# A recurrent time-mixing stage: another order on VectorE, three operations on GpSimd, and the last batch's end inside the stage behind it

## The chip, the core and the metric

The kernel runs on one core of a Trainium2 chip. A core has TensorE (PE in the profile, with PEld for its weight loads), VectorE (DVE), ScalarE (ACT), GpSimd (POOL) and a queue for transfers (SP), each with its own instruction stream; they meet only at semaphores. The metric is the device time of one launch in microseconds; the numbers below are medians of runs on the chip, and one execution was profiled.

## The reference

Two layers are computed for x of shape (4, 512, 128), which is 4 batches of 512 tokens with 128 channels:

```python
x = x + time_mix(layernorm(x))                 # RWKV-v4 recurrence, then W_out
x = x + transformer(layernorm(x))              # 6 layers: windowed attention and gated MLP
# time mixing: r, v, k = layernorm(x) @ W_rvk.T ; per channel, over the tokens t:
p = max(pp, u + k_t);   e1, e2 = exp(pp - p), exp(u + k_t - p)
y_t = (e1 * aa + e2 * v_t) / (e1 * bb + e2)
p2 = max(pp + w, k_t);  aa, bb, pp = exp(pp+w-p2)*aa + exp(k_t-p2)*v_t, ..., p2
out = (sigmoid(r) * y) @ W_out.T
```

The transformer part projects q, k and v for 16 heads, normalises and rotates q and k, attends in windows of 32 tokens, and runs a gated MLP; this is done 6 times.

## The kernel before

The program has two blocks of code, one behind the other, and every engine goes from the first to the second only when all engines have ended the first. The order of the instructions on each engine is written out by hand.

**The first block is time mixing.** It works on whole batches, with the 128 channels on the partitions and the 512 tokens along the free axis, so that one operation covers 128x512 elements in float32. For batch b VectorE normalises the rows (statistics, layer_norm), PE turns and projects them (turn_x, project), and ScalarE copies the results out (take_x, take_k, take_vr). Then VectorE runs three scans along the tokens, which are the recurrence: pp (scan_maximum, which also makes the exponents xd and yd), and bb and aa (scan_state, which first multiplies e2 by v into e2v). ScalarE makes e1, e2, f1 and f2 of the exponents (exponentials). The quotient takes six products and sums on VectorE (weigh_output: f2v, f1b, f1a, den, num and den again, with sigmoid's denominator er) and divide (a reciprocal and a product, rwkv). PE multiplies by W_out (output), VectorE adds x (residual, x_res), and the second LayerNorm follows: centre on PE, squares and a copy on ScalarE (take_centred), the variances on PE, an initial guess on VectorE (seed), Newton's steps on GpSimd (newton, twelve small operations), the widening to 128 columns on PE (widen), and a product on VectorE (scale_state) that leaves x_state[:, b], the transformer's input.

The batches are pipelined: pass b of VectorE's loop holds scale_state of b-2, scan_state of b, scan_maximum of b+1, residual of b-1, weigh_output of b, seed of b-1 and divide of b. GpSimd meanwhile splits the transformer's weights into two parts (w_hi and w_lo, one TENSOR_SCALAR and one TENSOR_TENSOR for each of the six chunks), and multiplies the rotation tables. In the loop it waits for the semaphore den2_ready before each split; this is given by the last operation of weigh_output, ahead of the reciprocal:

```python
for b in range(BATCH):                       # GpSimd, L302
    pool.wait_ge(den2_ready, b + 1)
    weights.split(pool, 0, 2 + b)
    newton(b - 1)
```

Behind the loop stands the end of the last batch, 3: scale_state(2), residual(3), the root on VectorE itself, scale_state(3) (L447 to L453), with centre and widen on PE.

**The second block is the transformer.** It goes in steps of 128 tokens of one batch in one layer, 4 steps for a batch, 96 steps and 10 more to empty the pipeline. A step projects six chunks of 512 columns on PE (V0, Q0, Q1, K0, K1, V1, three matmuls each, L1248 to L1250). For each q or k chunk, VectorE multiplies the bank by two tables (rotate, L921 and L928), ScalarE squares it (L1107), VectorE sums the squares (L938), and then there is one root for the whole step (L957 to L965). GpSimd adds the two products (L808) and normalises (L816). Scores, softmax, weighting, output projection and the MLP of earlier steps lie between them. In the first two steps those are not there yet. Batch 3 is first read in step 10.

## Time and profile before

| what | us |
|---|---|
| median of 3 runs (1739.13 to 1754.56) | 1740.24 |
| the profiled execution | 1745.12 |
| its span | 1743.3 |
| last operation of time mixing on VectorE ends | 102.47 |
| first projection of the transformer starts | 107.84 |

The profiled execution is 4.88 us above the median, and 1.82 us of it lie outside its span. Over the whole span PE is busy 91%, VectorE 83%, ScalarE 64% and GpSimd 60%. These are shares over both blocks: the first 108 us have limits of their own, and of the whole page only rows of that stretch tell about them.

### The profile page before, as it was taken

What the parts mean: (1) busy time and instruction counts of PE and PEld (TensorE: products, weight loads), DVE (VectorE), ACT (ScalarE), POOL (GpSimd) and SP (SyncE); (2) the same over time, 40 slices, a digit from 0 to 9 for tenths busy, and PEclk for the clock granted to TensorE, in tenths of its full rate; (3) what the DMA queues carried; (4) which work ended last, traced back from release to release, by engine and by line L of the source; (5) the groups of instructions that cost most, each with busy time, mean ns of one, the idle gap of its engine ahead of it and who ended that gap; (6) DMA issues with size and microseconds to landing.
All of it is one profiled execution on the core that took longest, in us unless ns stands there. A gap on an engine that the chain in (4) does not pass through costs nothing.

```text
span 1743.3 us, 77091 instructions
## 1 busy us (share of the span) xinstructions
PE 1585.1 (91%) x32733; PEld 1276.4 (73%) x32733; DVE 1445.9 (83%) x3193; ACT 1116.5 (64%) x2014; POOL 1049.6 (60%) x1028
## 2 busy tenths in 40 slices
PE   5358999999999999999999999999999999999985
PEld 2137878778778777778777787778777887787863
DVE  8758989888889888888888889888888888888851
ACT  5226667667667666667666666667666766776752
POOL 2236766666766665667566567576577585675530
PEclk8569999999999999999999999999999999999996
DMA  2011111111111111110211111211111211011110
GB/s 85 31 32 51 37 49 37 57 42 48 32 49 37 58 43 38 40 49 28 67 30 51 41 37 40 61 36 51 38 39 40 59 39 48 24 47 52 32 38 13
DMA packets 41083, 75.05 MB, mean 43 GB/s; under 512 B 9472, under 2 KB 22568, under 8 KB 40744
## 3 DMA queue, kind: packets, MB, share of 16 engines
q1 hardware_dynamic: 40744, 70.12, 13.9%
q8 instruction: 263, 4.31, 1.0%
q14 instruction: 76, 0.62, 0.1%
HBM read 20.08 MB, written 2.10 MB: 13 GB/s over the span
## 4 chain that ended last, share of the span: by engine, by line
PE 74%; issue 9%; DVE 5%; ACT 4%; POOL 3%; ACTq 0%; DVEq 0%; POOLq 0%
PE bank L1258 8%; PE bank L1248 8%; PE bank L1362 8%; PE bank L1295 7%; PE wide L1333 7%; PE bank L1250 7%; PE bank L1249 7%; PE bank L1348 5%; PE bank L1417 4%; PE bank L1313 4%; PE bank L1405 2%; PE bank L1284 2%; PE bank L1407 2%; PE bank L1406 2%; POOL qk L808 1%
## 5 line engine op out<-in xcount | busy, mean ns | idle before, releaser
L816 POOL TENSOR_TENSOR qk<-qk,rnorm 128x512 f32<-128x512 f32 x384 | 401.9, 1047 | 351.9 <-DVE rnorm L965 351.9
L808 POOL TENSOR_TENSOR qk<-qk,qk_sin 128x512 f32<-128x512 f32 x384 | 492.5, 1283 | 166.7 <-DVE qk_sin L928 166.5
L1107 ACT ACTIVATE squares<-bank 128x512 f32<-128x512 f32 x384 | 229.4, 598 | 153.8 <-DVE qk_sin L928 153.7
L938 DVE TENSOR_REDUCE norm<-squares 128x8 f32<-128x512 f32 x384 | 258.3, 678 | 31.0 <-ACT squares L1107 28.9
L1248 PE MATMUL bank<-w_hi,xs_hi 128*128 128x512 f32 x576 | 262.5, 456 | 16.1 <-ACT squares L1107 7.2
L921 DVE TENSOR_TENSOR qk<-bank,tables 128x512 f32<-128x512 f32 x384 | 261.7, 682 | 7.9 <-PE bank L1250 7.1
L928 DVE TENSOR_TENSOR qk_sin<-bank,tables 128x512 f32<-128x512 f32 x384 | 261.1, 680 | 0.6 <-POOL qk L808 0.6
L1250 PE MATMUL bank<-w_hi,xs_lo 128*128 128x512 f32 x576 | 230.7, 401 | 0.0
L1249 PE MATMUL bank<-w_lo,xs_hi 128*128 128x512 f32 x576 | 228.9, 397 | 1.4 <-issue 1.4
L1258 PE MATMUL bank<-ident,qk 128*128 128x128 f32 x1536 | 226.5, 278 | 3.3 <-POOL qk L816 2.0
L1258 PEld LDWEIGHTS bank<-ident,qk 128*128 128x128 f32 x1536 | 181.1, 142 | 42.8 <-issue 3.3
L1362 PE MATMUL bank<-o_t,w_o_s 128*128 128x128 f32 x1536 | 192.4, 279 | 2.8 <-DVE probs L979 1.9
L1295 PE MATMUL bank<-k_t,q_t 64*32 64x64 f32 x12288 | 152.1, 224 | 42.9 <-issue 42.6
L971 DVE TENSOR_REDUCE row_max<-bank 128x8 f32<-128x512 f32 x192 | 123.7, 686 | 75.8 <-PE bank L1295 74.4
L1362 PEld LDWEIGHTS bank<-o_t,w_o_s 128*128 128x128 f32 x1536 | 181.0, 193 | 6.0 <-issue 4.8
L1295 PEld LDWEIGHTS bank<-k_t,q_t 64*32 64x32 f32 x12288 | 143.0, 105 | 55.3 <-issue 50.5
L1333 PEld LDWEIGHTS wide<-v,p_t 64*32 64x32 f32 x12288 | 134.3, 105 | 61.9 <-issue 59.4
L1138 ACT COPY o_t<-bank 128x512 f32<-128x512 f32 x192 | 112.4, 585 | 97.7 <-PE bank L1348 97.3
L1333 PE MATMUL wide<-v,p_t 64*32 64x65 f32 x12288 | 165.8, 225 | 1.9 <-DVE o L992 1.1
L1099 ACT COPY v<-bank 128x512 f32<-128x512 f32 x192 | 113.9, 593 | 73.4 <-PE bank L1250 72.6
L1123 ACT ACTIVATE probs<-probs 128x512 f32<-128x512 f32 x192 | 121.1, 631 | 56.6 <-DVE probs L979 51.6
L1248 PEld LDWEIGHTS bank<-w_hi,xs_hi 128*128 128x128 f32 x576 | 109.5, 190 | 43.4 <-issue 16.2
(169 smaller groups left out, 2708.9 us busy)
## 6 DMA issues: line engine op xcount, KB each, us to landing
v<-v SPq DMA_DIRECT2D x96, 390.0 KB, 3.5
v<-v SPq DMA_DIRECT2D x72, 130.0 KB, 3.7
w_raw<-in_L_ffn_Wqkv SPq DMA_DIRECT2D x36, 256.0 KB, 3.8
w_o_s<-in_L_ffn_Wo SPq DMA_DIRECT2D x6, 512.0 KB, 5.6
w_raw<-in_L_ffn_W SPq DMA_DIRECT2D x6, 341.0 KB, 4.1
mix_x_nat<-in_L_attn_x SPq DMA_DIRECT2D x4, 256.0 KB, 3.3
x_res_scratch<-mix_x_res SPq DMA_DIRECT2D x4, 256.0 KB, 2.7
w_raw<-x_res_scratch SPq DMA_DIRECT2D x4, 256.0 KB, 3.7
```

Of the source, the lines that this page charges most:

```text
L808: pool.tensor_tensor(qk[:, g % 2, c, :], qk[:, g % 2, c, :], qk_sin[:, (QK_CHUNKS * g + c) % SINES, :], ALU.add).then_inc(added[c], 1)
L816: pool.tensor_tensor(view, view, rnorm[:, g % 2, c * HPC:(c + 1) * HPC].unsqueeze(2) .to_broadcast([P, HPC, DH]), ALU.mult).then_inc(norme ...
L921: dve.tensor_tensor(qk[:, g % 2, c, :].rearrange("p (h d) -> p h d", d=DH), src[:].rearrange("p (h d) -> p h d", d=DH), table(kind).unsque ...
L928: dve.tensor_tensor(qk_sin[:, (old + SINES) % SINES, :].rearrange("p (h a d) -> p h a d", a=2, d=DH // 2), src[:].rearrange("p (h a d) -> ...
L938: dve.tensor_reduce(norm2[:, c * HPC:(c + 1) * HPC], squares[:, c % 2, :].rearrange("p (h d) -> p h d", d=DH), AX.X, ALU.add).then_inc(sum ...
L1248: pe.matmul(bank_of(c)[:], l_hi, w_hi[:, n, :], start=True, stop=False)
L1249: pe.matmul(bank_of(c)[:], l_hi, w_lo[:, n, :], start=False, stop=False)
L1250: pe.matmul(bank_of(c)[:], l_lo, w_hi[:, n, :], start=False, stop=True).then_inc(projected[c], 1)
L1258: mm = pe.transpose(bank[2 + c % 2][:, j * P:(j + 1) * P], qk[:, g % 2, c, j * P:(j + 1) * P], ident[:])
L1295: mm = pe.matmul(bank[4 + r][WINDOW * h:WINDOW * (h + 1), col:col + 2 * WINDOW], q_t[row, pair, WINDOW * w:WINDOW * (w + 1)], k_t[row, pai ...
L1333: mm = pe.matmul(wide[WINDOW * h:WINDOW * (h + 1), w, quad * (DH + 1):(quad + 1) * (DH + 1)], p_t[row, r, 2 * s + m, WINDOW * h:WINDOW * ( ...
L1362: mm = pe.matmul(bank[4][:, 0:P], w_o_s[:, layer % 2, p, :], o_t[:, g % 2, p, :], start=(p == 0), stop=(p == PAIRS - 1))
```

## The change

Five things are done at once.

1. **VectorE's order.** A pass now begins with scan_state(b), then residual(b-1), scale_state(b-2), scan_maximum(b+1), layer_norm(b+2), the shorter weigh_output(b), seed(b-1) and divide(b). At the start, scan_maximum(0) moves ahead of the root and the normalising of batches 1 to 3. ScalarE runs exponentials(0) earlier, and take_centred before exponentials; PE runs centre before turn_x and project, and widen writes bank 7.
2. **Three operations on GpSimd.** f2v, f1a and num are made there (numerator), in front of the split, and the split no longer waits for den2_ready.
3. **The last batch's end moves.** output, residual, centre, variance, root, widen and scale_state of batch 3 leave the first block. They are written into steps 0 and 1 of the transformer (the functions with late_ in their names), and their root shares the instructions of step 0's root, 36 columns wide and no longer 32. The store of its x_res goes to SP's queue in step 1.
4. **Places.** Its tiles lie in the second half of the tables, in x_state and in qk_rows, so the writers of these (the tables and the rows of layer 1, and batch 3's shift) wait for the late semaphores.
5. **Other waits.** The scan bb waits for f1a of the batch before, and the copies into v_s, f1 and f2 wait for GpSimd's products.

```diff
@@ GpSimd, time mixing
+            def numerator(b):
+                p = b % 2
+                pool.wait_ge(f2_ready, b + 1)
+                pool.wait_ge(v_evac, b + 1)
+                pool.tensor_tensor(f2v[:], f2[:, p], v_s[:, p], ALU.mult).then_inc(f2v_ready, 1)
+                pool.wait_ge(f1_ready, b + 1)
+                pool.wait_ge(aa_ready, b + 1)
+                pool.tensor_tensor(f1a[:], f1[:, p], aa[:, p, 0:SEQ], ALU.mult).then_inc(f1a_ready, 1)
+                pool.wait_ge(f1a_ready, b + 1)
+                pool.wait_ge(f2v_ready, b + 1)
+                need(pool, rwkv_ready, b)
+                pool.tensor_tensor(num[:], f1a[:], f2v[:], ALU.add).then_inc(num_ready, 1)
...
             for b in range(BATCH):
-                pool.wait_ge(den2_ready, b + 1)
+                numerator(b)
                 weights.split(pool, 0, 2 + b)
                 newton(b - 1)
@@ VectorE, time mixing (weigh_output loses f2v, f1a and num)
-            statistics(NBLK, BATCH * NBLK)
-            layer_norm(1)
...
+            gather(NBLK, BATCH * NBLK)
             scan_maximum(0)
+            spread(NBLK, BATCH * NBLK)
+            layer_norm(1)
             for b in range(BATCH):
+                scan_state(b)
+                residual(b - 1)
+                scale_state(b - 2)
+                scan_maximum(b + 1)
                 layer_norm(b + 2)
-                scale_state(b - 2)
-                scan_state(b)
-                scan_maximum(b + 1)
-                residual(b - 1)
                 weigh_output(b)
                 seed(b - 1)
                 divide(b)
-            b, p = BATCH - 1, (BATCH - 1) % 2
-            scale_state(b - 1)
-            residual(b)
-            dve.wait_ge(st_ready, b + 1)
-            seq(dve.tensor_scalar(var2[:, p], bank[7][:, 0:NBLK], EPS, None, ALU.add))
-            root(var2[:, p], rstd2[:, p], nt2[:, p], root_w[:, 0:NBLK], rs_ready)
-            scale_state(b)
-            dve.wait_ge(xl_ready, BATCH)
+            scale_state(BATCH - 2)
+            dve.wait_ge(rwkv_ready, BATCH)
+            dve.wait_ge(xl_ready, BATCH - 1)
@@ PE, time mixing
             for b in range(BATCH):
+                centre(b - 1)
                 turn_x(b + 2)
                 project(b + 2)
-                centre(b - 1)
                 output(b)
                 widen(b - 1)
...
-            centre(BATCH - 1)
-            widen(BATCH - 1)
@@ VectorE, transformer
+            def late_residual():
+                dve.wait_ge(late.o_ready, BATCH)
+                dve.tensor_tensor(late.x_res, bank[5][:], late.x_t, ALU.add).then_inc(late.res_ready, 1)
+            def late_var():
+                dve.wait_ge(late.st_ready, BATCH)
+                dve.tensor_scalar(norm2[:, NORMS:], bank[7][:, 0:NBLK], EPS, None, ALU.add).then_inc(late.seeded, 1)
+            def late_state():
+                dve.wait_ge(late.bc_ready, BATCH)
+                dve.wait_ge(late.cen_evac, 2 * BATCH)
+                dve.tensor_tensor(x_state[:, BATCH - 1, :], bank[7][:], late.xc, ALU.mult).then_inc(late.xl_ready, 1)
...
                 rotate(step, 1)
+                if step == 0:
+                    late_residual()
+                if step == 1:
+                    late_state()
...
                 sum_squares(step, 3)
+                if step == 0:
+                    late_var()
@@ ScalarE, transformer
                 square(step, 1)
+                if step == 0:
+                    late_centred()
@@ PE, transformer
+            def late_widen():
+                pe.wait_ge(late.seeded, BATCH)
+                pe.wait_ge(rooted, 1)
+                for j in range(NBLK):
+                    mm = pe.transpose(bank[7][:, j * P:(j + 1) * P],
+                                      rnorm[:, 0, NORMS + j:NORMS + j + 1].to_broadcast([P, P]), ident[:])
+                mm.then_inc(late.bc_ready, 1)
...
+                if step == 0:
+                    late_output()
                 weigh(step - 3, 1)
...
                 project(step, K0)
+                if step == 0:
+                    late_centre()
                 project(step, K1)
+                if step == 0:
+                    late_variance()
+                if step == 1:
+                    late_widen()
                 turn_qk(step - 1, 3, o_taken[1], step - 2)
```

Where the instructions stand now is seen at three places. The first is VectorE in the pass of batch 2, behind the product rwkv of batch 1; before, the rows are these (mix_x_res is residual, x_state<-wide is scale_state):

```order
L421 TENSOR_TENSOR x_state<-wide,mix_xc 128x512
L364 TENSOR_TENSOR mix_e2v<-mix_e,mix_v_s 128x512
L366 SCALAR_TENSOR_TENSOR mix_bb<-mix_e 128x512
L368 SCALAR_TENSOR_TENSOR mix_aa<-mix_e,mix_e2v 128x512
L350 SCALAR_TENSOR_TENSOR mix_pp<-mix_w_neg,mix_k_s 128x512
L354 SCALAR_TENSOR_TENSOR mix_xd<-mix_pp,mix_w_neg,mix_k_s 128x512
L357 SCALAR_TENSOR_TENSOR mix_yd<-mix_k_s,mix_first,mix_pp 128x512
L404 TENSOR_TENSOR mix_x_res<-bank,mix_x_t 128x512
L373 TENSOR_TENSOR mix_f2v<-mix_f,mix_v_s 128x512
L376 TENSOR_TENSOR mix_f1b<-mix_f,mix_bb 128x512
L378 TENSOR_TENSOR mix_f1a<-mix_f,mix_aa 128x512
L380 TENSOR_TENSOR mix_den<-mix_f1b,mix_f 128x512
```

On the same engine at the same place, the changed kernel has:

```order
L404 TENSOR_TENSOR mix_e2v<-mix_e,mix_v_s 128x512
L407 SCALAR_TENSOR_TENSOR mix_bb<-mix_e 128x512
L409 SCALAR_TENSOR_TENSOR mix_aa<-mix_e,mix_e2v 128x512
L439 TENSOR_TENSOR mix_x_res<-bank,mix_x_t 128x512
L456 TENSOR_TENSOR x_state<-wide,mix_xc 128x512
L390 SCALAR_TENSOR_TENSOR mix_pp<-mix_w_neg,mix_k_s 128x512
L394 SCALAR_TENSOR_TENSOR mix_xd<-mix_pp,mix_w_neg,mix_k_s 128x512
L397 SCALAR_TENSOR_TENSOR mix_yd<-mix_k_s,mix_first,mix_pp 128x512
L415 TENSOR_TENSOR mix_f1b<-mix_f,mix_bb 128x512
L418 TENSOR_TENSOR mix_den<-mix_f1b,mix_f 128x512
```

scale_state went from the head of the pass to behind the scans and residual, residual went ahead of scan_maximum, and f2v, f1a and num are gone.

The second place is GpSimd in the pass of batch 1; before, it held the split of one chunk and the Newton steps of batch 0, of which the first two operations are shown:

```order
L129 TENSOR_SCALAR w_hi<-w_raw 128x512
L131 TENSOR_TENSOR w_lo<-w_raw,w_hi 128x512
L291 TENSOR_TENSOR mix_nt<-mix_var,mix_rstd 128x4
L292 TENSOR_TENSOR mix_nt<-mix_nt,mix_rstd 128x4
L293 TENSOR_SCALAR mix_nt<-mix_nt 128x4
```

In the changed kernel the same pass of GpSimd is:

```order
L327 TENSOR_TENSOR mix_f2v<-mix_f,mix_v_s 128x512
L330 TENSOR_TENSOR mix_f1a<-mix_f,mix_aa 128x512
L334 TENSOR_TENSOR mix_num<-mix_f1a,mix_f2v 128x512
L129 TENSOR_SCALAR w_hi<-w_raw 128x512
L131 TENSOR_TENSOR w_lo<-w_raw,w_hi 128x512
L316 TENSOR_TENSOR mix_nt<-mix_var,mix_rstd 128x4
```

Three large operations came in front of the split, which now follows num and not the last operation ahead of the reciprocal.

The third place is VectorE in step 1 of the transformer, from the first rotation on (bank1 is the chunk Q0, then K0); before:

```order
L921 TENSOR_TENSOR qk<-bank1,tables 128x512
L928 TENSOR_TENSOR qk_sin<-bank1,tables 128x512
L921 TENSOR_TENSOR qk<-bank0,tables 128x512
L928 TENSOR_TENSOR qk_sin<-bank0,tables 128x512
L938 TENSOR_REDUCE norm2<-squares 128x8
```

In the changed kernel the engine has there:

```order
L962 TENSOR_TENSOR qk<-bank1,tables 128x512
L969 TENSOR_TENSOR qk_sin<-bank1,tables 128x512
L962 TENSOR_TENSOR qk<-bank0,tables 128x512
L969 TENSOR_TENSOR qk_sin<-bank0,tables 128x512
L1059 TENSOR_TENSOR x_state<-wide,x_state 128x512
L979 TENSOR_REDUCE norm2<-squares 128x8
```

late_state (L1059) came between the second rotation and the first sum of squares; it reads what late_widen writes on PE, which stands there behind the step's chunk K1.

## Rows read from the trace of the kernel before

**Rows 1.** Two stretches: length, busy PE, PEld, DVE, ACT, POOL, granted clock, DMA share, GB/s.

```profile
73.00:89.80 16.80, 6.87 (x16) 3.67 (x16) 12.61 (x15) 1.07 (x2) 4.28 (x14) 0.50 0.05 17
...
1000.00:1160.00 160.00, 151.75 (x3300) 125.20 (x3285) 138.90 (x302) 108.84 (x197) 111.51 (x107) 1.00 0.15 45
```

**Rows 2.** VectorE's waits between 20 and 103 us: total, times, longest.

```profile
DVE x_state L421 <- PE wide L593: 10.3, 4, 3.0
...
DVE mix_var L412 <- PE wide L579: 4.1, 3, 1.9
```

**Rows 3.** Timeline of one pass on VectorE: start, duration, engine, line, what.

```profile
52.74 0.69 DVE L394 TENSOR_TENSOR mix_rwkv<-mix_num,mix_rden 128x512 f32<-128x512 f32 x1
...
57.06 0.68 DVE L364 TENSOR_TENSOR mix_e2v<-mix_e,mix_v_s 128x512 f32<-128x512 f32 x1
...
62.47 0.68 DVE L404 TENSOR_TENSOR mix_x_res<-bank,mix_x_t 128x512 f32<-128x512 f32 x1
...
63.08 0.68 DVE L373 TENSOR_TENSOR mix_f2v<-mix_f,mix_v_s 128x512 f32<-128x512 f32 x1
...
68.91 3.35 DVE L390 RECIPROCAL mix_rden<-mix_den 128x512 f32<-128x512 f32 x1
...
72.29 0.69 DVE L394 TENSOR_TENSOR mix_rwkv<-mix_num,mix_rden 128x512 f32<-128x512 f32 x1
```

**Rows 4.** Timeline, GpSimd: the end of Newton's steps, and a split.

```profile
52.63 0.20 POOL L296 TENSOR_TENSOR mix_rstd<-mix_nt,mix_rstd 128x4 f32<-128x4 f32 x1
...
66.86 0.62 POOL L129 TENSOR_SCALAR w_hi<-w_raw 128x512 fp32r<-128x512 f32 x1 [14.02 <-DVE mix_den L386]
```

**Rows 5.** Single lines, first 110 us and all: duration in ns, least/median/most.

```profile
L131 POOL TENSOR_TENSOR w_lo<-w_raw,w_hi x6: 1262/1263/1272, 10.7 to 84.5; 128x512 fp32r<-128x512 f32 x6
...
L390 DVE RECIPROCAL mix_rden<-mix_den x4: 3340/3343/3352, 32.6 to 85.7; 128x512 f32<-128x512 f32 x4
```

**Rows 6.** Where GpSimd and VectorE work at once: timeline rows, then single lines.

```profile
18.14 1.64 POOL L138 TENSOR_TENSOR tables<-rot,qk_rows 128x256 f32<-128x256 f32 x1
17.67 1.59 DVE L350 TENSOR_TENSOR_SCAN mix_pp<-mix_w_neg,mix_k_s 128x512 f32<-128x512 f32 x1
19.30 1.03 DVE L354 SCALAR_TENSOR_TENSOR mix_xd<-mix_pp,mix_w_neg,mix_k_s 128x512 f32<-128x512 f32 x1
...
48.65 0.81 DVE L413 TENSOR_SCALAR mix_rstd<-mix_var 128x4 int32<-128x4 int32 x1
...
L138 POOL TENSOR_TENSOR tables<-rot,qk_rows x4: 719/776/1640, 16.0 to 18.1; 128x256 f32<-128x256 f32 x4
...
L350 DVE TENSOR_TENSOR_SCAN mix_pp<-mix_w_neg,mix_k_s x4: 1195/1197/1592, 17.7 to 59.9; 128x512 f32<-128x512 f32 x4
```

**Rows 7.** Timeline of the start: layer_norm of batch 1, and its k.

```profile
15.62 1.95 DVE L342 TENSOR_SCALAR mix_xn<-mix_x_nat,mix_mv,mix_rstd 128x128 f32<-128x128 f32 x4
...
21.31 0.59 ACT L472 COPY mix_k_s<-bank 128x512 f32<-128x512 f32 x1 [1.09 <-PE bank L563]
```

**Rows 8.** Timeline from the last quotient to the transformer's first projection.

```profile
89.10 0.69 DVE L394 TENSOR_TENSOR mix_rwkv<-mix_num,mix_rden 128x512 f32<-128x512 f32 x1
...
101.78 0.69 DVE L421 TENSOR_TENSOR x_state<-wide,mix_xc 128x512 f32<-128x512 f32 x1 [1.21 <-PE wide L593]
...
103.77 0.06 DVE L901 MEMSET xs<- 128x1 f32 x1 [1.30 <-PEq L193]
...
107.84 0.77 PE L1248 MATMUL bank<-w_hi,xs_hi 128*128 128x512 f32 x1 [6.10 <-POOL xs_lo L801]
```

**Rows 9.** Timeline: what the late operations cost before, and step 1's place.

```profile
73.04 2.08 PE L585 MATMUL bank<-mix_rwkv,mix_w_out_t 128*128 128x512 f32 x2 [4.44 <-DVE mix_rwkv L394]
...
74.91 1.06 PE L593 MATMUL wide<-ident,mix_rstd 128*128 128x128 f32 x4
...
124.20 0.68 DVE L938 TENSOR_REDUCE norm<-squares 128x8 f32<-128x512 f32 x1
...
124.97 0.80 PE L1248 MATMUL bank<-w_hi,xs_hi 128*128 128x512 f32 x1 [0.41 <-ACT squares L1107]
```

More of the change, by code:

```diff
@@ L139, in make_tables, with __init__ @@
                                row.unsqueeze(1).to_broadcast([P, NBLK, DH]), ALU.mult).then_inc(self.tables_ready, 1)
+class LateBatch:
+    def __init__(self, sem, weights, x_state, qk_rows):
+        spare = weights.tables[:, 1, :, :, :].rearrange("p k j d -> p (k j d)")
+        self.rwkv = self.xsq = spare[:, 0:SEQ]
+        self.x_res = spare[:, SEQ:2 * SEQ]
+        self.x_t = self.xc = x_state[:, BATCH - 1, :]
+        self.w_out_t = qk_rows[:, 1, 0:2, :].rearrange("p k d -> p (k d)")
+        self.o_ready, self.res_ready, self.cen_ready, self.cen_evac, self.st_ready = (
+            sem("m_" + name) for name in ("o_ready", "res_ready", "cen_ready", "cen_evac", "st_ready"))
+        self.seeded, self.bc_ready, self.xl_ready = (sem("m_" + name) for name in ("seeded", "bc_ready", "xl_ready"))
+        self.stored = [sem("m_stored0"), sem("m_stored1")]
 def load_rows(sp, qk_rows, q_scale, k_scale, layer, loaded):
@@ L271, in _ @@
             weights.load(sp, w_qkv, 0, 3)
-            for b in range(BATCH):
+            for b in range(BATCH - 1):
                 sp.wait_ge(res_ready, b + 1)
@@ L276, in _ @@
                     weights.load(sp, w_qkv, 0, 4 + b)
-            for done in stored:
-                sp.wait_ge(done, 16 * BATCH // 2)
+            sp.wait_ge(stored[0], 32)
+            sp.wait_ge(stored[1], 16)
         @block.gpsimd
@@ L376, in weigh_output @@
                 dve.tensor_tensor(f1b[:], f1[:, p], bb[:, p, 0:SEQ], ALU.mult).then_inc(f1b_ready, 1)
-                dve.wait_ge(aa_ready, b + 1)
-                dve.tensor_tensor(f1a[:], f1[:, p], aa[:, p, 0:SEQ], ALU.mult).then_inc(f1a_ready, 1)
+                dve.wait_ge(f2_ready, b + 1)
                 dve.wait_ge(f1b_ready, b + 1)
                 dve.tensor_tensor(den[:], f1b[:], f2[:, p], ALU.add).then_inc(den_ready, 1)
-                dve.wait_ge(f1a_ready, b + 1)
-                dve.wait_ge(f2v_ready, b + 1)
-                dve.tensor_tensor(num[:], f1a[:], f2v[:], ALU.add).then_inc(num_ready, 1)
                 dve.wait_ge(er_ready, b + 1)
@@ L393, in divide @@
                 need(dve, o_ready, b - 1)
-                dve.tensor_tensor(rwkv[:, b % 2], num[:], rden[:], ALU.mult).then_inc(rwkv_ready, 1)
+                dve.tensor_tensor(rwkv_of(b), num[:], rden[:], ALU.mult).then_inc(rwkv_ready, 1)
             def residual(b):
-                if not real(b):
+                if not finished_here(b):
                     return
@@ L1250, in project, with late_output, late_centre, late_variance @@
                 pe.matmul(bank_of(c)[:], l_lo, w_hi[:, n, :], start=False, stop=True).then_inc(projected[c], 1)
+            def late_output():
+                pe.matmul(bank[5][:], late.w_out_t, late.rwkv, start=True, stop=True).then_inc(late.o_ready, 1)
+            def late_centre():
+                pe.wait_ge(late.res_ready, BATCH)
+                pe.matmul(bank[6][:], center[:], late.x_res, start=True, stop=True).then_inc(late.cen_ready, 1)
+            def late_variance():
+                pe.wait_ge(late.cen_evac, 2 * BATCH - 1)
+                for j in range(NBLK):
+                    mm = pe.matmul(bank[7][:, j:j + 1], late.xsq[:, j * P:(j + 1) * P], mean_col[:], start=True, stop=True)
+                mm.then_inc(late.st_ready, 1)
+            def late_widen():
+                pe.wait_ge(late.seeded, BATCH)
+                pe.wait_ge(rooted, 1)
+                for j in range(NBLK):
+                    mm = pe.transpose(bank[7][:, j * P:(j + 1) * P],
+                                      rnorm[:, 0, NORMS + j:NORMS + j + 1].to_broadcast([P, P]), ident[:])
+                mm.then_inc(late.bc_ready, 1)
             def turn_qk(g, c, before, value):
```

100 lines of the change are left out of this document (64 added, 36 removed).

## Prediction

> **What bounds the kernel now.** I read the busy times by stretch first, since the page's shares mix two blocks with different limits. In the middle of the transformer PE is busy 151.75 of 160 us at a granted clock of 1.00; there the kernel is PE's. In the pass of time mixing that makes batch 3's quotient, VectorE is busy 12.61 of 16.8 us and PE 6.87, at a granted clock of 0.50, which is the level of 1.2 GHz [rows 1]. So the first 108 us belong to VectorE and to what it waits for. The change edits time mixing and two steps of the transformer, and the other steps keep their order: the time should move by two amounts, how much earlier the first projection starts (107.84 us before [rows 8]) and how much longer the first two steps take.
>
> VectorE's list of waits says where its first stage loses time: 10.3 us in four waits of scale_state for the widening on PE, and 4.1 us in three waits of seed for the variances [rows 2]. Behind the last quotient, which ends at 89.10 + 0.69 = 89.79 us, come 12.68 us for the end of batch 3 (last product at 101.78 + 0.69 = 102.47), then 5.37 us until the first projection [rows 8].
>
> **The walk without collisions.** I add VectorE's operations in the new order, by the distance between starts in one pass. From e2v to x_res there are six operations, e2v, bb, aa, pp, xd and yd, 62.47 - 57.06 = 5.41 us; a product or sum takes 63.08 - 62.47 = 0.61; the reciprocal up to rwkv takes 72.29 - 68.91 = 3.38 [rows 3]. A pass then holds 5.41, residual and scale_state 1.22, f1b and den and den again 2.0 (with their semaphores 0.05 each), seed 0.3, reciprocal 3.38, rwkv 0.6: 12.9 us, and 1.05 more where a layer_norm is in it (four operations like those that took 1.95 in rows 7, there slowed by tables that run beside them; I take the undisturbed half). The three moved operations are left out: 4 x 3 x 0.61 = 7.3 us less on VectorE in all.
>
> The waits of rows 2 have cover in the new order. The output matmul and the widening behind it end 75.97 - 72.98 = 3.0 us after the quotient (starts at 73.04 and 74.91, 1.06 long [rows 9]); scan_state and residual lie in front of scale_state and take 2.87 + 0.61 = 3.5. So the 10.3 us go but for the last one. Of seed's waits I say: the variances came some 6.2 us after residual began (62.47 to the reciprocal at 68.91, less seed itself [rows 3]). Between the two now stand residual, scale_state, scan_maximum's 2.56 and the 2.0, 5.8 us in all, so 0.3 or so of wait stays, and 2.9 in the last pass, which has no scan_maximum; collisions, next, fill this time. Newton's steps stay under the reciprocal: before they end at 52.83, with the next product at 52.74 [rows 4, 3].
>
> **What GpSimd's work costs VectorE.** Before, each split waits for den2_ready, and so lies under the reciprocal; there neither is slowed (the split's second operation takes 1262 to 1272 ns, the reciprocal 3340 to 3352) [rows 4, 5]. Now f2v, f1a, num and the split run freely beside VectorE's products. What that does is seen once before, at the tables: the scan that takes 1.20 took 1.59, since it started with a GpSimd operation under way; the next GpSimd operation, issued at 18.14 during the scan, took 1.64 and not 0.78, and the following operation of VectorE, at 19.30, took 1.03. A small tensor_scalar on SBUF took 0.81 beside a split at 48.65 [rows 6]. These are whole-instruction waits, on either side, and they alternate. I price a collision at the rest of the GpSimd operation: up to 1.2 us for one of 1.26, 0.55 for the split's first of 0.62 [rows 5, 4]. Operations of VectorE with one input, or one in a bank, I take as free of it, as the reciprocal was.
>
> No row before shows a plain tensor_tensor of two SBUF tiles beside such a GpSimd operation; the bounds are nothing (the reciprocal) and the full rest (the scan). I take the scan, which like f1b, den and e2v reads two tiles in SBUF. The Trainium skill has a rule that speaks against this change (SBUF — State Buffer, section "SBUF: two separate sides"): VectorE and GpSimd share a pair of ports, and an instruction of VectorE with two SBUF inputs, or in a two-port mode, and one of GpSimd that reads SBUF exclude each other for the whole instruction. By the rule every collision below counts; by the forms shown alone, those of e2v, f1b and den would fall away and the time would be some 3 us less.
>
> In a pass: f1a starts when aa is done and lies beside residual and scale_state, which read banks: nothing. num meets pp, and since xd waits for pp's end, num goes first and xd waits 1.2. The split's two operations come between xd and yd (0.55) and behind yd (1.2). f2v of the next batch comes out of GpSimd's queue when Newton's steps end, just behind rwkv, and e2v waits 1.15; this holds for batches 2 and 3, as there are no Newton steps ahead of batch 1's. Sum: 3.0 us for batch 1, 4.1 for 2 and 3.
>
> **The sum.** Start: batch 1's layer_norm ended at 17.57 [rows 7]. Now pp, xd and yd (2.56) stand ahead of it, four tables alternate with its root (1.7 more than before), and f2v of batch 0 takes 1.2: 23.0, and k of batch 1, at 21.31 + 0.59 = 21.90 before [rows 7], comes at 27.4. scan_state of batch 0 is done by then. From k on: 2.56 for pp, xd, yd, 1.05, 2.0, 4.0, and collisions of 4.0: batch 0's quotient ends at 41.0. Then 12.9 + 1.05 + 3.0 gives 58.0, 12.9 + 4.1 gives 75.0; the last pass has no scan_maximum (2.56 less) and 4.1 of collisions, 14.5: 89.5. So the quotients end where they did (89.79): order and offload gain what the collisions take. Behind that only widen and scale_state of batch 2 remain, 1.3 us: 90.8 for 102.47, that is 11.7 us earlier.
>
> Late operations in steps 0 and 1: late_output pushes PE's chunk Q1 by 1.9 us (it took 2.08 at 1.2 GHz [rows 9]); late_residual and late_var are 0.6 and 0.2 on VectorE; centre and variances lie partly in PE's waits for squares: step 0 grows by 2.0 to 3.5. In step 1 late_state stands ahead of the sum of squares that started at 124.20, and waits for K1 (from 124.97, 1.6 us at 1.2 GHz) and late_widen (1.06) [rows 9]: with its own 0.65 it ends at 128.25, 4.0 later, or 2.8 at 2.4 GHz. Queued behind it are VectorE's chunks K0 and K1 and the next root, and PE's V1 waits for them. About 0.6 to 1.2 of that was idle before: 1.5 to 3.5. Together 3.5 to 7, taken as 5. The store in SP's queue finds x_res done long before: nothing, or a fraction of a us if not.
>
> -11.7 + 5 = -6.7 us. The profiled execution (1745.12, span 1743.3) would become 1738.4; it lies 4.88 above the median of 1740.24, so the median comes to **1733.5 us**, 0.4% less. About 1% is what a measurement of this kernel tells from no change.
>
> **The rivals.** *No collisions*: products of two tiles pass GpSimd as the reciprocal does. Batch 1's layer_norm then ends at 17.57 + 2.56 = 20.1, its k comes at 24.5, batch 0's quotient ends 9.6 later at 34.1, and the passes take 14.0, 13.2 and 13.2 (the last waits 2.9 for seed). With the 1.3 us behind them the block ends at 75.8, 26.7 earlier: with the 5 us of the steps, -21.7 and 1718.5. For it: no plain product was ever seen blocked. Against it: the scan and the tensor_scalar were. *Half of them*: VectorE's operations without a semaphore between them keep ahead of GpSimd; half of some 17 us comes back, 1725. *Slower*: the other end of the same price. If every large GpSimd operation of the loop stops VectorE for its whole length, that is 4 x (3 x 1.26 + 0.62 + 1.26) = 22.6 us, and 3.1 for four tables: 25.7, against 21.7 that the change is worth without collisions. It decides at 21.7; the time would be 1744. Against it: f1a and Newton's steps meet operations that don't collide. A step 1 that stays at 1.2 GHz for longer would add to it.
>
> **How the numbers follow.** The forecast (1728 to 1741 by the bounds of the start, the steps and the collisions) has 0.55, half the collisions (1721 to 1728) 0.18, none (1713 to 1721) 0.19, slower than before 0.08. The range 1716 to 1741 leaves out half of the third case and the fourth. Faster by over 1% means below 1722.8: 0.19 and a quarter of the second case, 0.23. Slower by over 1%, above 1757.6, needs a fault that I don't see: 0.02. Within 1%: 0.75.
>
> **What would show it.** In the changed kernel's trace e2v, xd, yd, f1b and den last over 1 us in some passes, with a GpSimd operation ending inside each (right), or all stay at 0.68 (the first rival). The fourth quotient ends near 89.5 us, time mixing's last product near 91, the first projection starts near 96. scale_state in the loop waits for nothing. In step 1 late_state shows an idle time of 2 to 3.4 us that PE's widening ends. The rest of the steps, from the third on, keep their length; if these change, by the clock or otherwise, the sum is wrong from its frame on.

## The result, and the profile after

The changed kernel takes 1730.57 us (median of 7 runs, 1725.27 to 1734.06) beside 1744.79 us of the kernel before (7 runs, 1739.13 to 1754.56): a ratio of 0.9907, 95% interval 0.9882 to 0.9932, estimated from all the runs (the two medians alone give 0.9919). The forecast was 1733.5 us in a range of 1716 to 1741; the time fell by 14 us where the sum had 6.7.

The profiled execution of the changed kernel took 1725.56 us with a span of 1723.8. First the walk through time mixing and the first two steps, in the timeline of VectorE, GpSimd and PE (start, duration, engine, line, operation, tiles; in brackets the idle time ahead and what ended it):

```profile
37.98 0.69 DVE L429 TENSOR_TENSOR mix_rwkv<-mix_num,mix_rden 128x512 f32<-128x512 f32 x1
...
42.61 1.23 DVE L390 TENSOR_TENSOR_SCAN mix_pp<-mix_w_neg,mix_k_s 128x512 f32<-128x512 f32 x1
42.84 2.06 POOL L334 TENSOR_TENSOR mix_num<-mix_f1a,mix_f2v 128x512 f32<-128x512 f32 x1
43.88 1.57 DVE L394 SCALAR_TENSOR_TENSOR mix_xd<-mix_pp,mix_w_neg,mix_k_s 128x512 f32<-128x512 f32 x1
44.87 1.06 POOL L129 TENSOR_SCALAR w_hi<-w_raw 128x512 fp32r<-128x512 f32 x1
45.37 1.09 DVE L397 SCALAR_TENSOR_TENSOR mix_yd<-mix_k_s,mix_first,mix_pp 128x512 f32<-128x512 f32 x1
46.01 1.58 POOL L131 TENSOR_TENSOR w_lo<-w_raw,w_hi 128x512 fp32r<-128x512 f32 x1
46.39 2.06 DVE L382 TENSOR_SCALAR mix_xn<-mix_x_nat,mix_mv,mix_rstd 128x128 f32<-128x128 f32 x4
...
54.21 0.69 DVE L429 TENSOR_TENSOR mix_rwkv<-mix_num,mix_rden 128x512 f32<-128x512 f32 x1
54.26 1.77 POOL L327 TENSOR_TENSOR mix_f2v<-mix_f,mix_v_s 128x512 f32<-128x512 f32 x1
54.82 1.75 DVE L404 TENSOR_TENSOR mix_e2v<-mix_e,mix_v_s 128x512 f32<-128x512 f32 x1
...
63.50 1.58 POOL L131 TENSOR_TENSOR w_lo<-w_raw,w_hi 128x512 fp32r<-128x512 f32 x1
63.88 1.75 DVE L415 TENSOR_TENSOR mix_f1b<-mix_f,mix_bb 128x512 f32<-128x512 f32 x1
...
70.79 0.69 DVE L429 TENSOR_TENSOR mix_rwkv<-mix_num,mix_rden 128x512 f32<-128x512 f32 x1
...
76.72 1.59 POOL L334 TENSOR_TENSOR mix_num<-mix_f1a,mix_f2v 128x512 f32<-128x512 f32 x1
77.29 1.57 DVE L418 TENSOR_TENSOR mix_den<-mix_f1b,mix_f 128x512 f32<-128x512 f32 x1
...
84.37 0.69 DVE L429 TENSOR_TENSOR tables<-mix_num,mix_rden 128x512 f32<-128x512 f32 x1
...
91.07 0.77 PE L1319 MATMUL bank<-w_hi,xs_hi 128*128 128x512 f32 x1 [5.17 <-POOL xs_lo L840]
...
111.94 0.69 DVE L1059 TENSOR_TENSOR x_state<-wide,x_state 128x512 f32<-128x512 f32 x1 [3.12 <-PE wide L1340]
```

Three things are to be seen. xd, yd, e2v, f1b and den, which take 0.68 to 0.75 us when nothing is beside them, take 1.09 to 1.75 in the passes shown, each with a GpSimd operation of 128x512 ending inside it: the collisions are there. layer_norm (mix_xn), which has one tensor input and which the forecast took as free, is lengthened too: 2.06 for 1.10. The fourth quotient starts at 84.37 and not at 89.10 [rows 8]. The first projection starts at 91.07, 16.8 us ahead of 107.84 [rows 8].

VectorE's list of waits between 20 and 110 us (total, times, longest) answers to [rows 2]:

```profile
DVE qk L962 <- PE bank L1321: 6.5, 2, 5.2
DVE mix_pp L390 <- ACT mix_k_s L504: 1.7, 1, 1.7
DVE mix_var L447 <- PE wide L613: 0.8, 1, 0.8
...
DVE x_state L456 <- PE wide L628: 0.6, 1, 0.6
```

The 10.3 us of scale_state and the 4.1 of seed have become 0.6 and 0.8; the first line is the transformer's. The last of the four scale_states now stands in step 1 as late_state, outside this window, and waits 3.12 us there (the last row of the timeline above).

From the first projection on the gain shrinks: the first MLP contraction (hidden times w_2) starts at 232.33, before at 246.26, 13.9 us earlier (starts in the chain of work that ended last; in the timeline all are 0.16 to 0.17 us earlier). The busy times by stretch show the rest of the program, from that contraction to the 23rd in the chain of work that ended last, and from there to the end (length, busy time of PE, PEld, DVE, ACT, POOL, granted clock, DMA share, GB/s). First the kernel before:

```profile
246.26:1696.44 1450.18, 1382.08 (x29848) 1132.78 (x29848) 1239.48 (x2745) 982.87 (x1768) 929.12 (x877) 1.00 0.15 43
1696.44:1743.30 46.86, 28.05 (x213) 16.76 (x211) 8.52 (x22) 10.40 (x16) 2.49 (x2) 0.69 0.04 12
```

The same of the changed kernel:

```profile
232.33:1682.86 1450.53, 1379.91 (x29848) 1131.58 (x29848) 1238.10 (x2745) 982.67 (x1768) 929.01 (x877) 1.00 0.15 43
1682.86:1723.80 40.94, 22.07 (x213) 13.70 (x211) 8.51 (x22) 10.40 (x16) 2.49 (x2) 0.87 0.05 14
```

And of a second profiled execution of the same changed kernel, after_again below:

```profile
232.40:1677.22 1444.82, 1379.04 (x29848) 1130.80 (x29848) 1238.89 (x2745) 982.16 (x1768) 928.13 (x877) 1.00 0.15 43
1677.22:1723.60 46.38, 28.02 (x213) 17.36 (x211) 8.51 (x22) 10.40 (x16) 2.49 (x2) 0.68 0.04 12
```

The long stretch is the same in the first pair to 0.4 us. The end, 40.94 us beside 46.86, is not the change's: the second execution has it at 46.38, at a granted clock of 0.68. So the two profiled spans differ by 19.5 us, of which 13.9 stand at the first contraction and some 6 are the end's clock. Identical stretches vary by such amounts from execution to execution; in what follows the landmarks of the head (fourth quotient, first projection, first contraction) are the sharper measure, and the times only confirm. But each landmark is one execution's, and it carries the variation of the start: the kernel before, offload_only and late_only below have the same VectorE operations up to the first e2v, and start it at 23.50, 21.87 and 21.35. In the two executions of the changed kernel the first e2v differs by 0.33 us and the first projection by 0.36, so distances from the first e2v repeat. By that distance the first projection of the changed kernel comes 69.12 us behind the first e2v, before 84.34: 15.2 of the 16.8 us.

### The profile page after: what moved, and what is told of

It is laid out like the page before. It is cut to its first block, busy times and chain, and to the rows that moved or that the text cites. A ratio compares the mean times of both kernels' runs of the same rounds, so it can differ in the third digit from the quotient of the medians.

```text
span 1723.8 us, 77096 instructions
## 1 busy us (share of the span) xinstructions
PE 1572.6 (91%) x32733; PEld 1271.1 (74%) x32733; DVE 1445.5 (84%) x3173; ACT 1116.7 (65%) x2014; POOL 1070.7 (62%) x1040
## 4 chain that ended last, share of the span: by engine, by line
PE 74%; issue 9%; DVE 5%; ACT 4%; POOL 2%; ACTq 0%; DVEq 0%; POOLq 0%
PE bank L1350 8%; PE bank L1319 8%; PE bank L1456 8%; PE bank L1387 8%; PE wide L1427 7%; PE bank L1321 7%; PE bank L1320 7%; PE bank L1442 5%; PE bank L1511 4%; PE bank L1405 4%; PE bank L1376 2%; PE bank L1499 2%; PE bank L1501 1%; PE bank L1500 1%; PE bank L1467 1%
## 5 line engine op out<-in xcount | busy, mean ns | idle before, releaser
L1194 ACT COPY p_t<-bank 128x512 f32<-128x512 f32 x192 | 102.8, 591 | 60.4 <-PE bank L1405 60.3
```

## The experiments

My theory: the order and the late end win, by the waits of VectorE that they take away, and the offload loses, since three products of 0.61 us a pass leave VectorE but GpSimd's operations stop VectorE for more than that. The rival: the offload wins and the collisions are noise. A second question was why the first two steps grow. All landmarks are start times in the profiled execution of each kernel, in us. Each ratio is to the kernel before as it ran beside that kernel: its medians were 1744.30 beside order_only, offload_only, late_only and no_offload, 1743.98 beside state_later, f1a_only and the doses, 1748.62 beside best and after_again.

| kernel | 4th quotient | first projection | first contraction | median us | ratio, 95% |
|---|---|---|---|---|---|
| before | 89.10 | 107.84 | 246.26 | 1744.79 | 1 |
| changed | 84.37 | 91.07 | 232.33 | 1730.57 | 0.9907, 0.9882-0.9932 |
| order_only | 80.85 | 99.20 | 236.56 | 1734.80 | 0.9947, 0.9922-0.9972 |
| offload_only | 91.13 | 109.15 | 247.46 | 1748.15 | 1.0016, 0.9990-1.0042 |
| late_only | 87.10 | 94.11 | 235.51 | 1738.52 | 0.9973, 0.9948-0.9998 |
| no_offload | 80.20 | 88.78 | 229.37 | 1728.69 | 0.9915, 0.9887-0.9942 |
| state_later | 85.93 | 92.61 | 233.87 | 1731.09 | 0.9916, 0.9891-0.9942 |
| f1a_only | 78.33 | 86.55 | 228.48 | 1722.62 | 0.9884, 0.9861-0.9907 |
| dose_banks | 80.48 | 88.69 | 228.75 | 1730.48 (one run) | |
| dose_chain | 84.71 | 92.94 | 233.79 | 1736.08 (one run) | |
| best | 78.37 | 85.34 | 225.51 | 1722.86 | 0.9849, 0.9827-0.9872 |
| after_again | 84.03 | 90.71 | 232.40 | 1727.23 | 0.9882, 0.9861-0.9903 |

**One part alone.** Three kernels hold one part of the change each on top of the kernel before: its orders of VectorE, ScalarE and PE (order_only), the three products and the ungated split on GpSimd (offload_only), batch 3's end in the steps (late_only). Their edits are those pieces of the change's diff; the core of each stands here.

order_only (VectorE's part):

```diff
-                layer_norm(b + 2)
-                scale_state(b - 2)
                 scan_state(b)
-                scan_maximum(b + 1)
                 residual(b - 1)
+                scale_state(b - 2)
+                scan_maximum(b + 1)
+                layer_norm(b + 2)
```

> The kernel before with only the new order on VectorE, ScalarE and PE; no operation on GpSimd, and the last batch's end in the first block. My theory: the waits of scale_state and most of seed's go, and the start gives nothing: the first projection starts 6 to 10 us earlier than before (98 to 102). Rival, the order is worth nothing without the offload: within 2 us of before.

Measured: fourth quotient 8.25 us earlier, first projection 8.6 earlier, as my theory had it. From the first e2v (20.67) to the first projection it is 78.53 us for 84.34, 5.8 less; the other 2.8 lie ahead of it, and how much of them is the start's variation isn't shown.

offload_only (GpSimd's part; the three products leave VectorE's list):

```diff
-                pool.wait_ge(den2_ready, b + 1)
+                numerator(b)
                 weights.split(pool, 0, 2 + b)
```

> The kernel before with only the three operations on GpSimd (and the split behind them, not waiting for the last operation ahead of the reciprocal). Collision theory: f1a meets the scan pp and the products behind it here, since no operation on a bank follows aa; with num, the split and f2v VectorE loses 3.5 to 4.5 us a pass and saves 1.8: the first projection starts 4 to 9 us later than before (112 to 117), the kernel is 0.2 to 0.5% slower than before. Rival, no cost of collisions: 7 us earlier, 0.4% faster.

Measured: first projection 1.3 us later, where I had 4 to 9. But this execution was 1.6 us ahead before any offloaded operation ran. The timeline has the first e2v of the kernel before at

```profile
23.50 0.69 DVE L364 TENSOR_TENSOR mix_e2v<-mix_e,mix_v_s 128x512 f32<-128x512 f32 x1 [1.48 <-ACT mix_e L493]
```

and that of offload_only at

```profile
21.87 0.68 DVE L404 TENSOR_TENSOR mix_e2v<-mix_e,mix_v_s 128x512 f32<-128x512 f32 x1
```

From there to the first projection it took 87.28 us for 84.34, which is 2.9 more. The direction was right and the rival's gain of 7 is refuted; my price was too high. The time shows no difference (1.0016, 0.9990 to 1.0042).

late_only (VectorE's part; PE, ScalarE and SP get theirs likewise, and time mixing loses batch 3's end):

```diff
+                if step == 0:
+                    late_residual()
+                if step == 1:
+                    late_state()
                 maximum(step - 2, 0)
```

> The kernel before with only the last batch's end moved into steps 0 and 1. My theory: 10 to 11 us less until the first projection (97 to 98), and 4.8 us more in the first two steps, as in the changed kernel: 5 to 6 us faster in all, 0.3%. Rival, the two steps take back all of it: no difference from before.

Measured: from the fourth quotient's start to the first projection 94.11 - 87.10 = 7.0 us, where it was 18.74 [rows 8]: 11.7 less, where I had 10 to 11. The first projection came 13.7 earlier because this execution was already 2.15 us ahead at its first e2v (21.35), which is not the late end's doing. In the time 5.8 us are left of it, as expected, the other steps' growth and the body's variation being in that too.

**All but the offload.** The products return to VectorE and the split waits for the denominator again:

```diff
-                numerator(b)
+                pool.wait_ge(den2_ready, b + 1)
                 weights.split(pool, 0, 2 + b)
```

> The changed kernel with f2v, f1a and num back on VectorE and each split waiting again for the last operation ahead of the reciprocal; the order and the late batch stay. Collision theory: the 12 operations cost VectorE 7.3 us again, some 12 us of collisions go (those of the tables stay), and about 4 us come back because Newton's steps now follow the split and the seed meets it: the first projection starts at 88 to 93 us (91.07 in the changed kernel), and the median is within 3 us of the changed kernel's. Rival, the offload is what gained: the first projection starts at 98 us or later, and the kernel is 7 us slower than the changed one.

Measured: first projection at 88.78, 2.3 us ahead of the changed kernel, the fourth quotient 4.2 ahead, with 12 products more on VectorE. The groups by line and form between 20 and 92 us (busy us, mean ns of one) show that the collisions of these products are gone:

```profile
L404 DVE TENSOR_TENSOR mix_f1b<-mix_f,mix_bb 128x512 f32<-128x512 f32 x4 | 2.8, 688 | 0.0
...
L391 DVE TENSOR_TENSOR mix_e2v<-mix_e,mix_v_s 128x512 f32<-128x512 f32 x4 | 2.7, 682 | 0.0
```

In the changed kernel the same view gives:

```profile
L404 DVE TENSOR_TENSOR mix_e2v<-mix_e,mix_v_s 128x512 f32<-128x512 f32 x4 | 4.9, 1219 | 0.0
...
L415 DVE TENSOR_TENSOR mix_f1b<-mix_f,mix_bb 128x512 f32<-128x512 f32 x4 | 3.8, 946 | 0.0
```

So the offload costs 2.3 us at the head of this kernel, 1.3 alone on the old order (2.9 from the first e2v), and gains in neither. The times of the changed kernel and of no_offload can't be told apart; the landmarks can. Behind the quotient no_offload loses 2 us of its lead, because its last split, gated, pushes Newton's steps back (its last scale_state waits 2.11 us, the changed kernel's 0.60; used in best).

**Placed doses.** no_offload with three useless additions on GpSimd, at one place or at another:

```diff
+                if b > 0:
+                    pool.wait_ge(aa_ready, b + 1)
+                    pool.tensor_tensor(extra[:], mask_f[:, 0, :], mask_f[:, 1, :], ALU.add)
```

> no_offload with three useless additions of 128x512 numbers (two operands in SBUF, about 1.1 us each) put on GpSimd, one in each of passes 1, 2 and 3, issued when the scan of aa ends, beside VectorE's residual and scaling of the state (bank operands; in pass 1 the residual alone, so the addition reaches some 0.4 us into the scan of pp). My theory: first projection +0.3 to +0.9 us against no_offload's 88.78, and the bank operations keep 0.65-0.7 us. The rival, that any large GpSimd operation costs the same wherever it stands: as much as in dose_chain, +2.5 to +4.

```diff
+                if b < BATCH - 1:
+                    pool.wait_ge(pp_ready, b + 2)
+                    pool.tensor_tensor(extra[:], mask_f[:, 0, :], mask_f[:, 1, :], ALU.add)
```

> The same three additions on GpSimd, but issued in passes 0, 1 and 2 when the scan of pp ends, beside VectorE's xd and yd (both operands in SBUF). My theory: xd goes from 0.75 to about 1.6 us and yd from 0.75 to about 1.1 in each of three passes, 1.1-1.2 us a pass, and the first projection starts 3.0-3.6 us behind no_offload's 88.78, at 91.8-92.4. The rival, that waiting time elsewhere in the loop takes it up: less than +1.5.

Measured: dose_banks moves the first projection by -0.1 us, dose_chain by +4.2. Of the 4.2, 1.5 were there at the first e2v, ahead of any dose (22.36 beside 20.87); from that e2v to the fourth quotient dose_chain took 62.35 us and no_offload 59.33, which is 3.0 for three doses (2.7 to the first projection). dose_banks took 59.38 to the fourth quotient. The timeline of dose_chain beside one dose:

```profile
44.15 1.85 DVE L385 SCALAR_TENSOR_TENSOR mix_xd<-mix_pp,mix_w_neg,mix_k_s 128x512 f32<-128x512 f32 x1
...
44.19 1.26 POOL L331 TENSOR_TENSOR mix_extra<-mix_mask_f 128x512 f32<-128x512 f32 x1 [6.70 <-DVE mix_pp L381]
...
45.92 0.74 DVE L388 SCALAR_TENSOR_TENSOR mix_yd<-mix_k_s,mix_first,mix_pp 128x512 f32<-128x512 f32 x1
```

xd lasts 1.85 and not 0.75: it waits for nearly the whole addition, and yd behind it for nothing (I had spread the same sum over both). The timeline of dose_banks beside a dose in pass 1 and one in pass 2:

```profile
39.62 0.67 DVE L436 TENSOR_TENSOR mix_x_res<-bank,mix_x_t 128x512 f32<-128x512 f32 x1
39.78 1.26 POOL L331 TENSOR_TENSOR mix_extra<-mix_mask_f 128x512 f32<-128x512 f32 x1 [4.99 <-DVE mix_aa L400]
...
40.20 1.93 DVE L381 TENSOR_TENSOR_SCAN mix_pp<-mix_w_neg,mix_k_s 128x512 f32<-128x512 f32 x1
...
55.71 0.66 DVE L436 TENSOR_TENSOR mix_x_res<-bank,mix_x_t 128x512 f32<-128x512 f32 x1
...
55.87 1.27 POOL L331 TENSOR_TENSOR mix_extra<-mix_mask_f 128x512 f32<-128x512 f32 x1
...
56.52 0.69 DVE L453 TENSOR_TENSOR x_state<-wide,mix_xc 128x512 f32<-128x512 f32 x1 [0.15 <-PE wide L625]
```

Residual and scale_state, with one operand in a bank, keep 0.66 and 0.69 with the addition over them; in pass 1, which has no scale_state, the addition's end reaches the scan of pp, 1.93 for 1.22. That 0.7 us is why I expected +0.3 to +0.9; a wait of scale_state in pass 2 took it up (0.15 us, 0.57 in no_offload). The same operation costs 1.0 us or nothing, by what VectorE does beside it.

**One product of three.** f1a alone goes back to GpSimd, issued at the end of the scan of aa:

```diff
-                dve.tensor_tensor(f1a[:], f1[:, p], aa[:, p, 0:SEQ], ALU.mult).then_inc(f1a_ready, 1)
+                pool.wait_ge(f1_ready, b + 1)
+                pool.wait_ge(aa_ready, b + 1)
+                need(pool, num_ready, b)
+                pool.tensor_tensor(f1a[:], f1[:, b % 2], aa[:, b % 2, 0:SEQ], ALU.mult).then_inc(f1a_ready, 1)
```

> All three products of the numerator were back on VectorE in no_offload; here one of them alone, f1a = f1 x aa, is on GpSimd again, issued when the scan of aa ends, so that its 1.1 us run beside VectorE's residual and the scaling of the state, each of which reads one operand from a bank. My theory, that GpSimd stops only VectorE's operations with two operands in SBUF: these bank operations keep their 0.65-0.7 us, VectorE loses four products of 0.61 us, and the first projection starts 1.5-2.5 us ahead of no_offload's 88.78, at 86.3-87.3 (pass 0 has no bank operation to cover it and may lose some 0.5 us). The rival, that any large GpSimd operation costs VectorE about as much as it takes away: first projection within 1 us of 88.8 or later. Time 1726-1729 by the first, 1728.5-1731 by the second; the head's landmarks decide, since the time varies by more than that.

Measured: first projection at 86.55, 2.2 us ahead of no_offload, for four products of 0.61 taken from VectorE: the whole of it is kept but for the scan of pp in pass 1 (1.62 for 1.22). The time, 1722.62 us (4 runs), lies below the 1726 to 1729 I expected, and its interval overlaps that of no_offload: it shows nothing by itself. The timeline of pass 3, and in the last row the scaling behind the last quotient, which waits for the widening:

```profile
69.22 0.66 DVE L434 TENSOR_TENSOR mix_x_res<-bank,mix_x_t 128x512 f32<-128x512 f32 x1
69.43 1.09 POOL L331 TENSOR_TENSOR mix_f1a<-mix_f,mix_aa 128x512 f32<-128x512 f32 x1
70.50 0.69 DVE L451 TENSOR_TENSOR x_state<-wide,mix_xc 128x512 f32<-128x512 f32 x1 [0.62 <-PE wide L623]
...
81.14 0.69 DVE L451 TENSOR_TENSOR x_state<-wide,mix_xc 128x512 f32<-128x512 f32 x1 [2.10 <-PE wide L623]
```

**The growth of the first two steps.** The changed kernel with late_state moved behind the rotation of chunk 3 in step 1:

```diff
-                if step == 1:
-                    late_state()
                 maximum(step - 2, 0)
...
                 rotate(step, 3)
+                if step == 1:
+                    late_state()
```

> The changed kernel with one move: on VectorE the last batch's final product (bank times centred state, tile x_state) stands behind the rotation of chunk 3 of step 1, no longer ahead of it. In the changed kernel's trace VectorE idled 3.12 us ahead of it for TensorE's four transposes, and the rotations of step 1 stood behind. My theory, that a strict order on VectorE makes the fill 4.8 us longer and that 3 us of it is this one wait: the second root goes from 26.6 us behind the first projection to 23.5-24.5, the first MLP contraction from 232.3 to 229-230.5 us, the time falls by 2-3 us (1727-1729 at the changed kernel's median of 1730.6). The rival, that the fill is bound by the transposes and copies on TensorE and ScalarE that the late steps add: VectorE only waits later, the second root stays within 1 us of 26.6, and the first contraction within 1 us of 232.3.

Measured: the second root starts at 116.01, 23.4 us behind the first projection, so the wait of 3.12 us is gone from there, as my theory had it. But VectorE then waits in the next step instead, 2.70 us where the changed kernel waits 0.97, as the timeline of state_later shows:

```profile
116.01 0.18 DVE L1000 TENSOR_SCALAR norm<-norm 128x32 f32<-128x32 f32 x1
...
120.69 0.69 DVE L962 TENSOR_TENSOR qk<-bank,tables 128x512 f32<-128x512 f32 x1 [2.70 <-PE bank L1321]
```

and the first contraction comes 233.87 - 92.61 = 141.26 us behind the first projection, which is what the changed kernel has (232.33 - 91.07 = 141.26), and the time is the same. My theory failed where it counts: that wait bounded nothing. The rival was right on the contraction and wrong on the second root, which it wanted unmoved. That PE bounds the fill in its place is what the next wait suggests, and isn't shown further.

**The version the runs point to.** f1a_only with Newton's steps ahead of the last split:

```diff
+                if b == BATCH - 1:
+                    newton(b - 1)
                 pool.wait_ge(den2_ready, b + 1)
                 weights.split(pool, 0, 2 + b)
-                newton(b - 1)
+                if b < BATCH - 1:
+                    newton(b - 1)
```

> The order and the late end of the change, of the offload only the one product that is free (f1a beside the bank operations), each weight split under VectorE's reciprocal, and in the last pass GpSimd's Newton steps ahead of the last split instead of behind it. In f1a_only VectorE's last scaling of the state waited 2.10 us for the transposes behind that Newton chain. My theory: Newton runs under the reciprocal and ends 1.9 us earlier, the split runs beside a bank operation and nothing else, and the first projection starts at 84.4-85.2 instead of 86.55; against the changed kernel (91.07) that is 6-6.5 us at the head, of which the longer fill leaves all, so 1723-1726 where the changed kernel gives 1730. The rival: the last split, now behind the last product, holds up the end of the block on GpSimd, and the first projection stays within 0.5 us of 86.55.

> The changed kernel once more, timed beside the best one on the same chip: 1728-1732, and 5-8 us above it if the head's landmarks are what counts; the rival, that the times of the two can't be told apart since the body alone varies by some 6 us between executions, would show as medians within 2 us.

Measured: 1722.86 us (5 runs) beside 1727.23 of the changed kernel (4 runs) and 1748.62 of the one before (11 runs, 1735.54 to 1750.49) on the same chip; the intervals of best and of the changed kernel overlap a little (0.9872, 0.9861). The first projection starts at 85.34, 1.2 us ahead of f1a_only and 5.4 ahead of after_again: a little short of the 84.4 to 85.2 I expected. The changed kernel's median lies 4.4 us above best's, under the 5 to 8 I expected and over the 2 of the rival. In the timeline the split is now the last to end, at 79.62 + 1.27 = 80.89, behind VectorE's last product (79.63 + 0.69 = 80.32), as the rival of best had it; whether it holds up the block isn't shown:

```profile
78.23 0.20 POOL L321 TENSOR_TENSOR mix_rstd<-mix_nt,mix_rstd 128x4 f32<-128x4 f32 x1
...
79.62 1.27 POOL L131 TENSOR_TENSOR w_lo<-w_raw,w_hi 128x512 fp32r<-128x512 f32 x1
79.63 0.69 DVE L454 TENSOR_TENSOR x_state<-wide,mix_xc 128x512 f32<-128x512 f32 x1 [0.57 <-PE wide L626]
```

In time best and f1a_only can't be told apart.

## Why the prediction was right, and where its sizes were off

**The end of time mixing.** The forecast had its last product ending at 102.47 before and 11.7 us earlier after. The piece on which this rests, the end of batch 3 out of the way, came as computed: from the fourth quotient to the first projection 18.74 us before, 7.0 in late_only, 6.7 in the changed kernel. Its last product ended at 85.66 + 0.69 = 86.35, 16.1 us earlier; the 4.4 beyond the forecast are the quotient's, next. The cover for the waits of [rows 2] came too.

**Order and offload.** "So the quotients end where they did" was the step that failed in size: forecast 41.0, 58.0, 75.0 and 89.5, measured (start plus 0.69) 38.67, 54.90, 71.48 and 85.06. The term that was mis-sized is the collisions. For the four passes I had 4.0, 3.0, 4.1 and 4.1 = 15.2 us; the lengthened operations sum to 2.0 (pp, xd, yd), 2.1 (xd, yd, layer_norm), 3.5 (e2v, pp, xd, yd, f1b) and 2.2 (e2v, den, den again) = 9.8. Their places were right in passes 1 and 2. For pass 0 the forecast gives no parts of its 4.0; num and the split cost 2.0 there, and the next f2v fell under the reciprocal. In pass 3, which has no scan of pp, there is no xd or yd to be stopped; there I had charged num and both halves of the split although nothing stood beside them but den and den again. These 5.4 us, and 0.8 at the start (k of batch 1 came at 26.6 and not at 27.4), came out as 4.4 at the last quotient; small waits (residual 0.5, seed 0.8) and wider gaps between operations took the rest.

That the products of two SBUF tiles are stopped at all was the open point of the forecast, for no row before showed one. They are: 1.75 for 0.68. The rule of the Trainium skill (SBUF — State Buffer, section "SBUF: two separate sides"), that a VectorE instruction with two SBUF inputs and a GpSimd instruction that reads SBUF shut each other out for the whole instruction, agrees with what the doses measured: xd 1.85 beside an addition of 1.26, bank operands 0.66 and 0.69 beside the same. One sentence of the forecast is wrong, that operations with one input are free: layer_norm was stopped for 0.96, and the same working had already put its 1.95 [rows 7] down to the tables beside it. The first rival (no collisions, 1718.5) is refuted, and so is the slower one, which had every large GpSimd operation stop VectorE for its whole length. The rival of half the collisions came near in size (9.8 of 15.2 us), but its reason isn't borne out: layer_norm stands behind yd without a semaphore between them and was stopped all the same.

**The parts.** The gain is the order's and the late end's: 8.6 us alone and 11.7 alone, 19.1 together in no_offload (16.4 from the first e2v). The offload took 2.3 of it back at the first projection (4.2 at the fourth quotient, where VectorE's 12 products less, 7.3 us, stand against the collisions). The offload is two edits in one, and no run parts them: the three products, and the split that no longer waits. By the operation that ends inside each lengthened one, the split accounts for 4.1 of the 9.8 us and the products for 5.7, with 1.0 more at the start, where f2v of batch 0 stops a step of the root. So the products alone would have about paid for themselves (6.7 against 7.3), and the ungated split is what tips the balance; this is read from the trace and not tested.

**The first two steps.** I had 3.5 to 7 and took 5. At the second root it was that: 26.62 us behind the first projection for 21.90, 4.7 more. But the sum carried it on to the end, and by the first contraction part of it was gone. From first projection to first contraction the nine kernels with the late end take 140.1 to 141.9 us, the three without 137.4 to 138.4: means 141.0 and 138.0, so 3.0 (2.8 for the changed kernel). Step 0 grew by 1.3 us at its root (12.65 for 11.39), where I had 2.0 to 3.5 at 1.2 GHz: PE's granted clock was 0.50 in 92 to 96 us and 1.00 in 96 to 100, from 4.9 us behind the first projection on, with PE busy without a gap before; in the kernel before PE had gaps and the clock was still 0.50 in 113 to 116, up to 8.2 us behind. That the earlier rise paid for part of the late work isn't tested. The sum for step 1 counted late_state's wait as time; the wait was there (3.12 us, forecast 2 to 3.4), but state_later shows that VectorE waits there in place of waiting for PE later. What makes up the 3.0 is not shown; that it is the late operations on PE in these steps (late_output 1.91, late_centre 1.12, variances 1.05, late_widen 1.05) is only argued.

**The frame.** "The rest of the steps keep their length" held: 1450.53 beside 1450.18 us. So the sum at the first contraction is -16.77 + 2.84 = -13.93, where I had -11.7 + 5 = -6.7. The mechanism was right, and the amount only half of what came: -13.9 lies nearer to the 15 us of half the collisions (1725) than to the forecast, though some 2 us of it may be the late start of the kernel before in its profiled execution. That the forecast still lies within 3 us of the time is luck: the 1740.24 from which it was worked is the median of the first three of the seven runs, whose median is 1744.79, and these 4.6 us hid most of the 7.2 that the sum missed.

## What to carry to other kernels

Work moved to GpSimd is priced by what VectorE does beside it, not by its length: the same 1.1 to 1.3 us cost VectorE nothing beside operations with a bank operand or the reciprocal, and about 1.0 when they ran alone beside products of two SBUF tiles, more than the 0.61 that an offloaded product saves. So gate GpSimd's operations on the moments where VectorE runs the harmless forms. Landmarks of single executions are to be read from a point that the change can't move: here the start alone varied by some 2 us. And a wait that a change introduces is worth only what no later wait behind it would have taken; moving it away is a cheap test.

## What the runs showed of the hardware that I had not expected

When GpSimd has several operations queued, the two engines alternate: a collision can cost VectorE less (xd +0.82 and yd +0.35 in the changed kernel) than a lone one does (xd +1.10 in dose_chain), but the next operations are hit as well (layer_norm +0.96, f1b +1.07). Small GpSimd operations lose to VectorE's products and scans: in f1a_only the last four Newton steps of 128x4 numbers, 0.20 us each under the reciprocal, took 0.52, 0.52, 0.98 and 1.04 in pass 2 beside rwkv, e2v, bb and aa, of which the last three kept their 0.68, 1.22 and 1.19. The same code at the end of the program ran at a granted clock of 0.87 in one execution of the changed kernel and 0.68 in another, a difference of 5.4 us in 46.
